# Linear attention, softmax attention and a mixture of experts on one core: key differences in the score ring, visits between maxima, groups added by GpSimd

## The reference, cut to what matters

```
h = layernorm(x, ln1_g, ln1_b)
q, k, v = h @ Wq, h @ Wk, h @ Wv            # 4096 tokens, 16 heads of 16
scores = q . k / sqrt(16)                   # per head 4096 x 4096
attn = softmax(scores, axis=-1)
ctx = attn . v
```

## Time and profile before

| | |
|---|---|
| three runs, median | 3849.7 us (3828.7 to 3851.27) |
| the profiled execution: its own time | 3834.31 us |
| its span | 3832.6 us |
| TensorE busy | 3510.3 us, 92% |
| VectorE busy | 2884.1 us, 75% |
| ScalarE busy | 2607.7 us, 68% |
| GpSimd busy | 738.1 us, 19% |
| mean granted TensorE clock, share of full | 0.948 |
| exponentials L760, 2048 of 128x1024 | 2056.3 us |
| reductions L794, 3584 of 128x512 | 2249.6 us |

### The profile page before, as it was taken

The page is one execution under the profiler, slowest core; times in us unless marked ns, Lnnn a source line. Parts: engine busy times, 40 slices in busy tenths (PEclk is TensorE's granted clock), DMA queues, the critical chain, the costliest instruction groups (busy, mean ns, idle before and its releaser), DMA issues. The chain is left out here.

```text
span 3832.6 us, 85440 instructions
## 1 busy us (share of the span) xinstructions
PE 3510.3 (92%) x29108; PEld 1904.7 (50%) x29108; DVE 2884.1 (75%) x5446; ACT 2607.7 (68%) x3034; POOL 738.1 (19%) x735
## 2 busy tenths in 40 slices
PE   7979999999999999999999999999998708999980
PEld 4534444444444444444444444444443607999980
DVE  1768999999999999999999999999994512333335
ACT  2428888888888888888888888888886104555540
POOL 0300000000000000000000000000000367888856
PEclk9959999999999999999999999999999658999995
DMA  3630101011010101101010110101001434344424
GB/s 108 222 64 15 25 15 27 14 28 24 17 26 15 27 14 28 25 15 26 15 28 13 28 26 15 26 15 28 13 15 66 164 110 138 137 137 137 137 90 128
DMA packets 172197, 210.89 MB, mean 55 GB/s; under 512 B 62464, under 2 KB 136064, under 8 KB 166656
## 3 DMA queue, kind: packets, MB, share of 16 engines
q1 hardware_dynamic: 153424, 177.96, 17.1%
q0 software_dynamic: 6336, 16.79, 1.4%
q10 hardware_dynamic: 12144, 12.06, 0.9%
HBM read 135.64 MB, written 71.04 MB: 54 GB/s over the span
## 5 line engine op out<-in xcount | busy, mean ns | idle before, releaser
L760 ACT ACTIVATE probs<-s_ps 128x1024 f32<-128x1024 f32 x2048 | 2056.3, 1026 | 409.8 <-PE s_ps L679 382.8
L794 DVE TENSOR_REDUCE unit_max<-m_ps 128x1 f32<-128x512 f32 x3584 | 2249.6, 685 | 58.2 <-PE m_ps L671 58.1
L694 PE MATMUL o_ps<-probs,v_here 128*32 128x256 f32 (+1 forms) x15360 | 1285.1, 407 | 0.5 <-ACT probs L760 0.5
L679 PE MATMUL s_ps<-q_stage,k_ring 50*128 50x512 f32 x4096 | 1026.0, 493 | 0.5
L671 PE MATMUL m_ps<-k_ring,q_stage 48*128 48x512 f32 x3840 | 963.8, 421 | 42.9 <-DMA q_stage<-qs_dram 22.1
L679 PEld LDWEIGHTS s_ps<-q_stage,k_ring 50*128 50x128 f32 x4096 | 384.7, 184 | 767.1 <-issue 650.3
L671 PEld LDWEIGHTS m_ps<-k_ring,q_stage 48*128 48x128 f32 x3840 | 620.3, 188 | 159.2 <-DVE unit_max L794 133.8
L694 PEld LDWEIGHTS o_ps<-probs,v_here 128*32 128x32 f32 x15360 | 303.4, 108 | 506.5 <-issue 503.5
L615 POOL TENSOR_TENSOR neg_max<-no_max,tile_max 128x4 f32<-128x4 f32 x127 | 25.5, 201 | 2450.8 <-DVE tile_max L809 2450.8
L1527 DVE TENSOR_TENSOR hidden_low<-h_ps,hidden_high 128x512 fp32r<-128x512 f32 x184 | 127.3, 692 | 366.3 <-ACT hidden_high L1491 366.3
L1487 ACT ACTIVATE h_ps<-h_ps,b_here 128x512 f32<-128x512 f32 x184 | 121.4, 660 | 255.2 <-PE h_ps L1424 255.2
(11 more groups left out here) (181 smaller groups left out, 2407.1 us busy)
## 6 DMA issues: line engine op xcount, KB each, us to landing
w_in<-in_W SPq DMA_DIRECT2D x46, 1024.0 KB, 4.9
q_stage<-qs_dram SPq DMA_DIRECT2D x768, 32.0 KB, 1.8
k_ring<-ks_dram SPq DMA_DIRECT2D x96, 128.0 KB, 4.2
slots_dram<-zero_rows SPq DMA_DIRECT2D x24, 512.0 KB, 6.4
rows_e<-slots_dram SPq DMA_DIRECT2D x24, 512.0 KB, 3.9
y_slots_dram<-y_out ACTq DMA_DIRECT2D x23, 512.0 KB, 4.2
qs_dram<-parts SPq DMA_DIRECT2D x16, 512.0 KB, 2.9
ks_dram<-parts SPq DMA_DIRECT2D x32, 256.0 KB, 2.7
```

The source lines that it names most:

```text
L679: last = nc.tensor.matmul(s_ps[:, t % 2, k, :], k_ring[at:at + AROWS, par, P * t:P * t + P], q_stage[at:at + AROWS, buf * CHUNK:buf * CHUN ...
L694: last = nc.tensor.matmul(o_ps[at:at + SQ, lo:hi], v_here[:, par, first_tile(t) + 2 * k, :], probs[:, t, k, lo:hi], start=(pair == 0), sto ...
L760: nc.scalar.activation(probs[:, t, :, :], s_ps[:, t % 2, :, :], ACT.Exp).then_inc(exp_done, 1)
L794: nc.vector.tensor_reduce(unit_max[:, b, qt, 2 * j + k:2 * j + k + 1], m_ps[:, block_of(t, k) % 3, :], AX.X, ALU.max).then_inc(m_read, 1 + ...
```

## The change

Constants: `DIFFS = 2` units of differences per chunk stand in the score ring behind units 5 and 8 (`DIFF_AT`), so the ring has 18 units per chunk. A unit of differences is 128 queries (query tile u = 0 or 1) x 512 differences on both sides; `kd_ring` holds 2 x 512 differences per head (keys of block 0 of a side minus keys of block 1 of the same side) instead of 2048, at both partition offsets. ScalarE takes one Relu of 128x1024 of it; then two "partner" blocks of `m_ps` are each added and reduced by VectorE's fused operation. Maxima: 12 plain pairs (24 reductions) and 2 partner pairs (4 fused operations) in 28 blocks instead of 32. `DIFF_CHUNKS = 4` of the 8 chunks of the first stage make differences.

Visits: 14 instead of 15, the first and the last wide, 12 narrow, and their places are written out by hand in TensorE's `chunk`. `turn_o` and `gather` are gone: SyncE copies three of the four groups of `o_here` to partitions 0 to 16 (`align`), GpSimd adds the four with three operations (`sum_o`), and `store` has two DMAs. ScalarE's copy of `o_ps` stands behind unit 3 instead of 8 and also waits for the sum of the chunk before (`o_summed`). VectorE's copy to `ctx_stage` is gone. ScalarE's and VectorE's loops are written out.

```diff
-VISITS = ((0, 0, CHUNK),) + tuple((p, lo, lo + HALF) for p in range(1, UNITS // 2) for lo in (0, HALF))
-SLOTS = tuple(range(10, 25))
-COPY_SLOT, TURN_SLOT = 8, 10
-RELU_PAIRS = (1, 3)
-FINISH_SLOTS = (0, 2)
+VISITS = ((0, 0, CHUNK),) + tuple((p, lo, lo + HALF) for p in range(1, 7) for lo in (0, HALF)) + ((7, 0, CHUNK),)
+PLAIN = (2, 3, 6, 7, 8, 9, 10, 11, 12, 13, 14, 15)
+BLOCKS = 2 * (UNITS - DIFFS)
+PARTNER_AT = (12, 20)
+RING_UNITS = UNITS + DIFFS
+DIFF_AT = (6, 10)
...
+            def align(n):
+
+                sp.wait_ge(o_copied, n + 1)
+                for g in range(1, P // SQ):
+                    sp.dma_start(o_groups[:, g - 1, :], o_here[SQ * g:SQ * g + O_COLS, :]).then_inc(o_aligned, 16)
...
                 if loads:
+                    sp.wait_ge(s_done, i * RING_UNITS + (LEAD * DIFFS + score_at(0) + 1))
                     load_q(sp.snap(h + n // CHUNKS), n % CHUNKS, n % Q_BUFS)
+                if before:
+                    align(i - 1)
                 if ahead:
                     rows(i + 1, (qc + 1) % Q_BUFS)
                 if more and qc == 0:
                     load_head(sp.snap(h + 1), sp.snap((h + 1) & 1))
                 if before:
+                    store(i - 1, sp.snap(h - 1) if qc == 0 else h, (qc - 1) % CHUNKS)
...
+            def sum_o(n):
+
+                pool.wait_ge(o_aligned, n * (16 * (P // SQ - 1)) + 16 * (P // SQ - 1))
+                pool.wait_ge(ctx_out, n * (2 * 16) + 2 * 16)
+                nc.gpsimd.tensor_tensor(ctx_stage[:, :], o_here[0:O_COLS, :], o_groups[:, 0, :], ALU.add).then_inc(o_added, 1)
+                pool.wait_ge(o_added, n * 2 + 1)
+                nc.gpsimd.tensor_tensor(ctx_stage[:, :], ctx_stage[:, :], o_groups[:, 1, :], ALU.add).then_inc(o_added, 1)
+                pool.wait_ge(o_added, n * 2 + 2)
+                nc.gpsimd.tensor_tensor(ctx_stage[:, :], ctx_stage[:, :], o_groups[:, 2, :], ALU.add).then_inc(o_summed, 1)
...
+            def differences(n, u):
...
+                if at_ring > 1:
+                    pe.wait_ge(s_read, at_ring - 1)
+                for k, at in enumerate((0, TOP_ROW)):
+                    last = nc.tensor.matmul(s_ps[:, at_ring % 2, k, :], q_stage[at:at + SROWS, col:col + P],
+                                            kd_ring[at:at + SROWS, par, :], start=True, stop=True)
+                last.then_inc(s_done, 1)
+
+            def max_block(n, b, k, t):
...
+                if g >= 3:
+                    pe.wait_ge(m_read, g - 2)
...
+            def chunk(i):
+                n = i + LEAD
...
+                scores(i, 0)
+                plain(n, 0)
+                scores(i, 1)
+                if i > 0:
+                    values(i - 1, 10)
+                if i > 0:
+                    values(i - 1, 11)
+                scores(i, 2)
+                plain(n, 1)
+                if i > 0:
+                    values(i - 1, 12)
+                scores(i, 3)
+                plain(n, 2)
+                if i > 0:
+                    values(i - 1, 13)
+                plain(n, 3)
+                scores(i, 4)
+                scores(i, 5)
+                values(i, 0)
+                plain(n, 4)
+                differences(n, 0)
+                values(i, 1)
+                scores(i, 6)
+                plain(n, 5)
+                values(i, 2)
+                scores(i, 7)
+                partners(n, 0)
+                scores(i, 8)
+                values(i, 3)
+                plain(n, 6)
+                differences(n, 1)
+                values(i, 4)
+                scores(i, 9)
+                plain(n, 7)
+                values(i, 5)
+                scores(i, 10)
+                plain(n, 8)
+                scores(i, 11)
+                values(i, 6)
+                partners(n, 1)
+                scores(i, 12)
+                values(i, 7)
+                plain(n, 9)
+                scores(i, 13)
+                scores(i, 14)
+                plain(n, 10)
+                values(i, 8)
+                scores(i, 15)
+                plain(n, 11)
+                values(i, 9)
...
+            def differences(n, u):
...
+                nc.scalar.activation(excess[:, u, :, :], s_ps[:, diff_place(n, u) % 2, :, :], ACT.Relu).then_inc(s_read, 1)
...
             def copy_o(i):
                 act.wait_ge(pv_done, i * len(VISITS))
+                act.wait_ge(o_summed, i)
                 nc.scalar.activation(o_here[:, :], o_ps[:, :], ACT.Copy).then_inc(o_copied, 1)
 
+            def chunk(i):
+                for t in range(4):
+                    exponential(i, t)
+                if i > 0:
+                    copy_o(i)
+                for t in range(4, 6):
+                    exponential(i, t)
+                differences(i + LEAD, 0)
+                for t in range(6, 9):
+                    exponential(i, t)
+                differences(i + LEAD, 1)
+                for t in range(9, UNITS):
+                    exponential(i, t)
...
+            def partners(n, u):
+
+                dve.wait_ge(s_read, diff_place(n, u) + 1)
+                for k in range(2):
+                    g, j = n * BLOCKS + PARTNER_AT[u] + k, 1 - k
+                    dve.wait_ge(m_done, g + 1)
+                    dve.sem_inc(dve_passed, 1)
+                    nc.vector.tensor_tensor_reduce(excess[:, u, j, :], m_ps[:, g % 3, :], excess[:, u, j, :], 1.0, LEAST,
+                                                   ALU.add, ALU.max, unit_max[:, n % 2, u, 2 * j:2 * j + 1]).then_inc(m_read, 1)
```

More of the change, by code:

```diff
@@ L697, in values @@
                 last.then_inc(pv_done, 1)
-            def turn_o(it, c):
-                pe.wait_ge(o_copied, it * PAIR + c)
-                pe.wait_ge(m_read, it * (PAIR * RING_BLOCKS) + ((c + LEAD) * RING_BLOCKS + TURN_BLOCK - 2))
-                for t in range(TPC):
-                    last = nc.tensor.matmul(m_ps[SQ * t:SQ * t + SQ, TURN_BLOCK % 3, 0:P], gather[:, :],
-                                            o_here[:, P * t:P * t + P], start=True, stop=True)
-                last.then_inc(o_turned, 1)
@@ L708, in chunk @@
-            def chunk(it, c, ahead):
-                if ahead:
-                    load_waits(it, c + LEAD)
-                pe.wait_ge(rows_in, (it * PAIR + (c + 1)) * ROW_DMAS)
-                for t in range(UNITS):
-                    scores(it, c, t)
-                    if ahead:
-                        max_pair(it, c + LEAD, t)
-                    for visit, slot in enumerate(SLOTS):
-                        if slot == t:
-                            values(it, c, visit)
-                        if slot == t + UNITS and c > 0:
-                            values(it, c - 1, visit)
-                    if t == TURN_SLOT and c > 0:
-                        turn_o(it, c)
@@ L740, in _ @@
+            for n in range(LEAD):
+                maxima_alone(n)
+            for i in range(RING):
+                chunk(i)
+            for visit in range(10, len(VISITS)):
+                values(RING - 1, visit)
         @block.scalar
@@ L772, in _ @@
+            for n in range(LEAD):
+                for u in range(DIFFS):
+                    differences(n, u)
+            for i in range(RING):
+                chunk(i)
             copy_o(RING)
@@ L833, in _ @@
-            chunk(0, 0, finish=False, turn=False)
-            chunk(1, 1, turn=False)
-            chunk(2, 0, turn=False)
-            chunk(3, 1)
-            chunk(4, 0)
-            chunk(5, 1, stores=1)
-            with dve.Fori(3, RING // 2) as it:
-                for b in range(2):
-                    chunk(dve.snap(it * 2 + b), b, stores=it + (b - 2))
-            chunk(RING, 0, ahead=False, stores=RING // 2 - 2)
-            chunk(RING + 1, 1, ahead=False, finish=False, stores=RING // 2 - 1)
@@ new lines, in chunk @@
+            def chunk(n):
+                for r in range(2):
+                    plain(n, r)
+                if n > 0:
+                    tile_maxima(n - 1)
+                for r in range(2, 4):
+                    plain(n, r)
+                if n > 0:
+                    turn_maxima(n - 1)
+                for r in range(4, 6):
+                    plain(n, r)
+                partners(n, 0)
+                for r in range(6, 9):
+                    plain(n, r)
+                partners(n, 1)
+                for r in range(9, 12):
+                    plain(n, r)
@@ L847, in row_statistics @@
+            for n in range(RING):
+                chunk(n)
+            tile_maxima(RING - 1)
+            dve.wait_ge(rows_in, (RING - 1) * ROW_DMAS)
+            turn_maxima(RING - 1)
 def row_statistics(nc, dve, ch, stats, mean_var, std, rstd, var_ready, std_ready, n):
```

347 lines of the change are left out of this document (166 added, 181 removed).

## The result

The changed kernel takes 3686.47 us (median of four executions, 3682.15 to 3691.94), the kernel before 3845.61 us beside it: a ratio of 0.9603 (95% interval 0.9583 to 0.9624), 4% faster. (A ratio is taken over fast executions alone, so where executions scatter it need not be the quotient of the two medians.) The prediction was 3685. The profiled execution took 3691.94 us (span 3690.2), the longest of its four; so 142.4 us of span are to be explained.

A forecast was written before the change was run, and what follows sets the result against it. TensorE's own order was taken as the bound, plus 0.9 us of waits a chunk. 126 chunks x (20.93 - 19.75) = 149 us; 3834.3 less 149 and 2.6, plus 1, gives 3684, stated as 3685; range 3620 to 3800.

The forecast's parts named there:

- TensorE's work, 20.01 to 19.03: TensorE's matmuls per chunk without waits: fewer runs of visits and no `turn_o` save 0.98 us.
- Waits, 0.9 to 0.72: TensorE's waits per chunk: 0.9 us on VectorE before; after, slips in the walk to 19.68 plus 0.07 for maxima banks.
- The walk: Written order stepped through one chunk with ScalarE: closes at 19.68 us, 19.75 with banks; 3640 to 3740 has 0.60.
- s1, s9 and s11: Score units 1, 9 and 11 of a chunk, starts said to slip behind ScalarE by 0.17, 0.03 and 0.17 us.
- Rival 2: Maxima banks slip: reductions at 0.63, four pairs each costing 0.2 us more, 20.5 us a chunk, 3780; chance 0.10.
- Groups, done at 14 us into the chunk: Group DMAs land by 9 us, GpSimd's three adds take 5, done at 14; the next copy needs it at 25.
- SP's order: SyncE's queue: `align` ahead of `rows` starts row DMAs at about 7 us, not 5; hidden by the chunk's length.
- Once only: Outside steady chunks: first maxima 2 x 1.3 us less, first head 1.3 later, stage one 2 less, tail net 0.
- 1: TensorE's work alone, ScalarE slips don't occur: 19.0 us per chunk, 240 less, 3595; chance 0.05.
- 3: Code loading: written-out ScalarE and VectorE code stops its engine for loads, 84 us come back, 3770; chance 0.12.
- 4: Joining visits saves nothing, waits only move; only `turn_o` and a little go: 20.7 us a chunk, 3805; chance 0.06.
- 5: GpSimd's adds stop VectorE, which then needs 22.1 us: +1.2 x 126, 3985, slower; chance 0.07.

The follow-up runs named there:

- the second experiment: Kernel before, loops written out, `turn_o` replaced by group DMAs (behind the key loads) and GpSimd's adds, copy of `o_ps` still at unit 8: 4009.22 us, ratio 1.0396.
- two other kernels with the same order on TensorE: The changed kernel with three further GpSimd adds a chunk (3686.76 us), and with 32 rows in each group DMA instead of 17 (3679.88 us).
- third experiment: Kernel before, loops written out, GpSimd's sum for `turn_o`, copy at unit 8, group DMAs issued ahead of the key loads: 3985.52 us, ratio 1.0337.

## Why the prediction came out right, and which of its terms did not

- **TensorE's work, 20.01 to 19.03**: right. `turn_o` alone is 0.22 to 0.26 us in the undisturbed chunks of the second experiment (0.33 said). One run more costs 0.44 with its waits (0.33 said). Joined and wide visits cost 1.00 (1.02 said). The 0.98 as a whole is 0.86 between the two kernels with halved reductions.
- **Waits, 0.9 to 0.72** (0.65 for scores, 0.07 for banks): the sum is right, its two terms are not. Measured are 0.21 for scores, at `scores` 14 only, and for banks 0.41 at `plain` 10 and 0.14 at `plain` 6, together 0.76. The walk took a unit of scores as readable after 0.6 us, where it is 0.55 (1562.00 to 1562.55, and 1522.44 to 1522.99 in the earlier trace rows), so s1, s9 and s11 don't slip. It took every block's reader as starting 0.42 us after the block. That holds for a pair behind another pair; behind a visit a reduction starts 0.54 after, and the fused operation, at the second partner pair, 0.67. So each bank comes free later than the walk had it, above all at `plain` 10, the pair that follows soonest on the one before. The two errors are 0.44 and 0.48 us a chunk with opposite signs: they cancel, so the 3685 owes part of its closeness to chance. Rival 2, banks that slip, is thus partly true, at two places with 0.55 us together instead of four at 0.2; I had named more than 0.5 us as its sign.
- **VectorE, 17.3**: 17.9. Eight reductions back to back take 5.03 us, (5.03 - 0.69)/7 = 0.62 each and not the 0.60 of the earlier trace rows; rival 2 had read 0.63 in the steady chunk and the walk didn't use it. **ScalarE, 18.5 and 94%**: 18.24, 92%. The walk's one idle spell of 0.3 us at s4 isn't there: the 1.5 us that ScalarE is idle come in pieces of 0.2 to 0.3, mostly waits for scores.
- **Groups, done at 14 us into the chunk**: they are done 11.5 us after the copy starts (1514.98 to about 1526.5), at 16 to 17. The landing was mis-sized (2 us said, 5 measured), and so were the issues (0.43 us each said, three in 1.87 measured); the adds were dearer in the sum than they are (1.6 said, 1.27 measured). What hides it holds: next copy 20 us after the last, 8 us to spare; nothing waits for the sum.
- **SP's order**: the maxima rows were said to start late behind `align`; they also wait in the DMA engines behind the groups (4.9 us instead of 1.5), which I had not seen. Both are covered. That `align` stands ahead of rows and keys I counted as a cost; it is what saves the change: behind them the ratio is 1.0000.
- **Loops 0**: confirmed, ratio 0.9989.
- **Once only**: the terms as listed are -2.6, +1.3 and -2, together -3.3, where the sum took -1.6; measured is -4.5 up to the first `tile_max`, within the scatter of that time. The tail was said to be 0 and is +5.
- **Rivals**: 1 (no slips, 3595) would need VectorE and ScalarE out of the way; even with half the reductions it is 3635. 3, 4 and 5 fell with the loops, the separated visits and the added adds; as to 3, after moved 93 packets of the second instruction queue and 188 of the first, before 89 and 204.

A chunk of after was 19.83 us in the profiled execution and 19.74 in two other kernels with the same order on TensorE. All of that is the second chunk, 31.61 us instead of some 22: the medians are 19.76, 19.76 and 19.75. Its cause is the clock at the start:
```profile
240.00:280.00 40.00, 39.90 (x153) 16.35 (x152) 29.87 (x59) 16.83 (x17) 0.55 (x3) 0.50 0.21 33
280.00:330.00 50.00, 50.00 (x424) 20.45 (x424) 41.79 (x80) 42.50 (x45) 9.28 (x15) 0.93 0.09 20
```
These windows of after have clock 0.50 and 0.93; the same two of the kernel with 32 rows have 0.69 and 1.00, with the same instructions on TensorE. Why one execution gets the higher level sooner than another stays open. That GpSimd's sum with the copy at unit 8 would fit with 32 rows in a transfer was not tried.

## What to carry to other kernels

Price an order on the bounding engine by its changes of kind as well as by its instructions, and then walk the buffers with each consumer's real start after its producer, one figure per kind of instruction and per what stands ahead of the producer: a sum that comes out right can hold two wrong terms. When work moves to an idle engine with an in-order queue, ask first when its input lands in the worst chunk (here the one with the key loads) and what stands behind it in that queue. Before a mean over many chunks is used, look whether one chunk makes it. Look at the number of rows of a small transfer as much as at its bytes.

## What the runs showed of the hardware

- Three transfers of 17 rows x 2 KB land 4.8 to 5 us after the last issue, even with nothing else under way; of 32 rows x 2 KB, mostly 1.4 to 1.6 us, up to 3.2. That the 17 rows go over a single DMA engine fits the rate in the tail and this run; no row names the engine.
- Beside the key loads such transfers took 6.2 to 8.5 us from the last issue when issued behind them, 10.3 to 11.4 when issued just ahead: being first in the queue doesn't protect them. In those two kernels the loads of key differences issued last are three of 128 KB. Behind the loads of after, whose last are six of 32 KB, the transfers took 4.9 us, as if alone.
- After stops of TensorE of 3.63 and 2.65 us (the second and third experiment) the granted clock fell to the 1.2 GHz level and stayed there for 20 us and for at least 30. With `align` last a stop of 4.79 us shows 0.69 in its own window and 0.97 in the 10 us after it, and (2918.3 - 241.5)/127 = 21.08 us is the mean chunk: 10 us more a head than after, twice the stop.
- A plain reduction starts 0.43 us after the start of its matmul pair when the pair stands behind another pair, 0.54 when it stands behind a visit (1516.74 to 1517.28). The fused add-and-maximum starts 0.57 us after in the first case (1579.21 to 1579.78), 0.67 in the second (1564.76 to 1565.43), so 0.13 later than a reduction in the same place.
